# Down projection of a gated MLP: one more pair of row tiles by seven block products

## The reference

```python
h = _L0_tok_ref(...)                                  # 16 x 128 x 1024
h = h + _L0_attn_ref(_layernorm(h), ...)
h = h + _L0_ffn_ref(_layernorm(h), ...)

def _qlinear(x, q, scale, A, Bm):
    w = (q.astype(jnp.float32) - Q_ZERO) * (scale * Q_STEP)[:, None]
    return jnp.einsum('bsh,oh->bso', x, w) + LR_SCALE * (x @ A @ Bm)
g, u = _qlinear(x, gate...), _qlinear(x, up...)       # 2752 hidden features
return _qlinear(silu(g) * u, down...)                 # back to 1024
```

## Time and profile before

| | us |
|---|---|
| median of 3 runs | 1879.42 |
| lowest, highest | 1877.77, 1879.56 |
| the profiled execution's own time | 1879.99 |
| its span | 1878.2 |
| TensorE busy in the span | 1779.6 |
| VectorE busy | 1310.0 |
| GpSimd busy | 977.1 |
| ScalarE busy | 741.9 |

### The profile page before, as it was taken

The page is one execution under the profiler, slowest core; times in us unless marked ns, Lnnn a source line. Parts: engine busy times, 40 slices in busy tenths (PEclk is TensorE's granted clock), DMA queues, the critical chain, the costliest instruction groups (busy, mean ns, idle before and its releaser), DMA issues.

```text
span 1878.2 us, 31695 instructions
## 1 busy us (share of the span) xinstructions
PE 1779.6 (95%) x12772; PEld 970.3 (52%) x12772; DVE 1310.0 (70%) x1758; ACT 741.9 (40%) x1065; POOL 977.1 (52%) x683
## 2 busy tenths in 40 slices
PE   0897999999999999999999999999999999999999
PEld 0786565665666656545554344444444444444444
DVE  8885677777787887855656866775665555377775
ACT  4694334334433444422114544544444443112221
POOL 6881334434334344522360576675668776468672
PEclk9998999999999999999999999999999999999999
DMA  2232111210122221144432333343546453633531
GB/s 100 54 87 68 45 58 17 66 36 21 49 76 65 77 61 62 68 156 166 163 117 79 101 109 127 108 128 101 180 146 207 150 164 104 229 106 141 175 116 68
DMA packets 102705, 194.93 MB, mean 104 GB/s; under 512 B 14304, under 2 KB 75488, under 8 KB 92064
## 3 DMA queue, kind: packets, MB, share of 16 engines
q1 hardware_dynamic: 102560, 192.90, 32.1%
HBM read 135.72 MB, written 56.11 MB: 102 GB/s over the span
## 4 chain that ended last, share of the span: by engine, by line
PE 75%; DVE 10%; POOL 3%; issue 2%; ACT 2%; DMA 0%; DVEq 0%; ACTq 0%
PE acc L1572 13%; PE acc L1574 13%; PE acc L1740 9%; PE acc L1705 4%; PE ps_p L1364 4%; PE ps_p L1366 3%; PE ps_p L1365 3%; PE acc L1478 3%; PE acc L1480 3%; PE acc L1479 3%; PE ps_t L1391 3%; PE ps_p L1380 2%; PE ps_p L1381 2%; PE ps_p L1382 2%; PE ps_l L1581 2%
## 5 line engine op out<-in xcount | busy, mean ns | idle before, releaser
L1218 POOL TENSOR_TENSOR prob<-prob,mx 128x1024 f32<-128x1024 f32 x64 | 121.4, 1898 | 365.6 <-DVE mx L2169 365.6
L1364 PE MATMUL ps_p<-x_hi,w_qk 128*128 128x512 f16 x512 | 194.7, 380 | 0.0
L1365 PE MATMUL ps_p<-x_lo,w_qk 128*128 128x512 f16 x512 | 194.0, 379 | 0.0
L1366 PE MATMUL ps_p<-x_hi,w_qk 128*128 128x512 f16 x512 | 194.0, 379 | 0.0
L1271 POOL TENSOR_TENSOR hidden<-up,hidden 128x512 f16<-128x512 f32 x80 | 91.1, 1161 | 142.3 <-ACT hidden L1998 142.1
L1223 POOL TENSOR_TENSOR prob<-prob,sm 128x1024 f32<-128x1024 f32 x64 | 120.2, 1897 | 52.9 <-DVE sm L2176 52.9
L1380 PE MATMUL ps_p<-w_v,x_hi 128*128 128x256 f16 x512 | 140.4, 274 | 4.1 <-PEq L916 2.8
L1832 ACT ACTIVATE pth<-ps_t 128x512 f16<-128x512 f32 x128 | 76.1, 595 | 163.8 <-PE ps_t L1391 163.7
L1381 PE MATMUL ps_p<-w_v,x_hi 128*128 128x256 f16 x512 | 140.3, 274 | 0.0
L1382 PE MATMUL ps_p<-w_v,x_lo 128*128 128x256 f16 x512 | 140.3, 274 | 0.0
L2421 DVE SCALAR_TENSOR_TENSOR up<-acc,gu_scale,up 128x512 f32<-128x512 f32 x120 | 90.0, 750 | 61.5 <-PE acc L1574 61.0
(11 more groups left out here) (399 smaller groups left out, 4546.1 us busy)
## 6 DMA issues: line engine op xcount, KB each, us to landing
q_raw<-in_gu_q SPq DMA_DIRECT2D x42, 1024.0 KB, 6.2
hid_parts<-hidden_parts SPq DMA_DIRECT2D x16, 1376.0 KB, 7.0
hidden_parts<-hidden SPq DMA_DIRECT2D x42, 512.0 KB, 3.5
down_raw<-in_down_q SPq DMA_DIRECT2D x22, 512.0 KB, 3.6
w_raw<-in_w_qk SPq DMA_DIRECT2D x8, 1024.0 KB, 4.8
h_tokens<-n_tok SPq DMA_DIRECT2D x16, 512.0 KB, 3.7
o_parts<-ot SPq DMA_DIRECT2D x32, 256.0 KB, 2.3
wv_raw<-in_w_o SPq DMA_DIRECT2D x8, 1024.0 KB, 4.9
```

What stands on the lines that cost most here:

```text
L1218: nc.gpsimd.tensor_tensor(prob[s % 2][p][:], prob[s % 2][p][:], bc(mx[p][:], H, 2), ALU.subtract).then_inc(s_sub[p], 1)
L1364: nc.tensor.matmul(out[:], w[:, j % 2, m, 0, at], xn_hi[:, k, tok], start=(k == 0), stop=False)
L1365: nc.tensor.matmul(out[:], w[:, j % 2, m, 0, at], xn_lo[:, k, tok], start=False, stop=False)
L1366: last = nc.tensor.matmul(out[:], w[:, j % 2, m, 1, at], xn_hi[:, k, tok], start=False, stop=(k == KT - 1))
```

## The change

`PLAIN_PAIRS` becomes 1. Row tiles 2 and 3 leave the plain rows and become the first seven-product pair, q = 1, ahead of the six that were there. On GpSimd pair 0 now runs `residual_and_term(0)`, `hid_one(1)`, `hid_three(1)`, `residual_and_term(1)`. On ScalarE the four `down_term` of rows 0 and 1 stand ahead of the high parts of the hidden sums. On VectorE `level_sum(2)` moves ahead of `add_first(0)` and of the hidden sums, and `level_sum(4)` stands right behind `scale_sums(1)`.

```diff
-PLAIN_PAIRS = 2
+PLAIN_PAIRS = 1
@@ GpSimd
         for q in range(DP):
             sums = PLAIN_PAIRS <= q + 1 < DP
+            if q < PLAIN_PAIRS:
+                residual_and_term(2 * q)
             if sums:
                 hid_one(q + 1, 0)
                 hid_one(q + 1, 1)
-            residual_and_term(2 * q)
+            if q >= PLAIN_PAIRS:
+                residual_and_term(2 * q)
@@ ScalarE
             down_term(2 * q, 1)
+            if q < PLAIN_PAIRS:
+                down_term(2 * q + 1, 0)
+                down_term(2 * q + 1, 1)
             if sums:
                 high_hid_sum(q + 1, 0, f1[:], s_f1, 2)
                 high_hid_sum(q + 1, 1, f2, s_f2, 1)
-            down_term(2 * q + 1, 0)
-            down_term(2 * q + 1, 1)
+            if q >= PLAIN_PAIRS:
+                down_term(2 * q + 1, 0)
+                down_term(2 * q + 1, 1)
@@ VectorE
-        for n in range(2):
-            scale_sums(n)
-            add_first(n)
+        scale_sums(0)
+        dve.wait_ge(s_half, 1)
+        for i in range(KD):
+            dve.wait_ge(s_l3, i + 1)
+            tt(level_sum(2, i), level_sum(3, i), level_block(0, 0, i), ALU.add).then_inc(s_l2, 1)
+        add_first(0)
         sum_two_hid(PLAIN_PAIRS)
         sum_two_low(PLAIN_PAIRS)
         low_hid_sum(PLAIN_PAIRS, 0, f1[:])
         low_hid_sum(PLAIN_PAIRS, 1, f2)
-        scale_sums(2)
-        add_first(2)
-        dve.wait_ge(s_half, 1)
-        for i in range(KD):
-            dve.wait_ge(s_l3, i + 1)
-            tt(level_sum(2, i), level_sum(3, i), level_block(0, 0, i), ALU.add).then_inc(s_l2, 1)
-        scale_sums(3)
+        scale_sums(1)
         for i in range(KD):
             dve.wait_ge(s_l2, i + 1)
             tt(level_sum(4, i), level_block(1, 0, i), level_sum(2, i), ALU.subtract).then_inc(s_l4, 1)
-        add_first(3)
+        add_first(1)
```

## The result

| | us |
|---|---|
| before, median of 12 runs | 1878.51 |
| after, median of 12 runs | 1884.26 |
| ratio, 95% interval | 1.0029, 1.0021 to 1.0037 |
| profiled execution after: span | 1881.5 |

One of the twelve executions after took 3796 us; it is counted in the median and left out of the ratio. The changed kernel is slower by 5.75 us in the medians. The interval of the ratio, times 1878.5, is 3.9 to 7.0 us. The two profiled spans are only 3.3 us apart, because this execution reached the down stage 2.06 us earlier: the chain's first 32 matmuls of the stage start at 1591.35, against 1593.41 before.

What follows compares the result with a forecast made beforehand. TensorE, busy 95% of the span, was taken as the bound. Saving 4.3 us, p7 starting 10.0 later (+5.7), and +0.3 for store and clock gave +6.0 on 1879.42: 1885.4 us, range 1877.5 to 1890.0.

Steps and rivals of the forecast that it cites:

- the walk: Engine lists followed through the new first pair to p7: 10.0 us later, less 4.3 saved; +4 to +8 us, chance 0.48.
- The saving of 4.3 us: TensorE, down stage: two plain rows of 38.10 us replaced by one seven-product pair of 33.79, if nothing waits.
- Turns one to one: VectorE's level sums alternate with GpSimd's adds, 1.54 us a turn: level_sum(2) takes 13.7 us, level_sum(4) 8.5, not 3.5 each.
- The wait before p22: TensorE in the new pair stands 6.9 us for scale_sums(1), ready at 1644.1 where p22 wanted it at 1637.2.
- The wait before p7: TensorE stands another 3 us for VectorE's read v at 1661.6; about 1.4 if the clock falls after the first stall.
- the slow clock: TensorE's clock falls after the first stall, costing about 1.5 us, absorbed because p7 waits for VectorE anyway.
- the late store: Row 1's later store may hold x22, which writes the same buffer: at most +0.7 us, within +0.3 shared with the clock.
- a second fall: TensorE's clock falls again after the wait before p7, which would add its cost; within +0.3 us shared with the store.
- The adds are not held up: Rival: level_sum(2) and level_sum(4) take 3.5 us each, nothing waits, 1875.1 us; chance 0.13.
- partly held up: Rival: two VectorE adds per turn, level_sum(2) about 8.5 us, level_sum(4) 5.5; 1877, up to 1880 us; chance 0.21.
- GpSimd goes first: Rival: level_sum(2) and level_sum(4) run only after GpSimd's lists, 1888.1 us; chance 0.18 shared with clock and store.

Runs made afterwards that it cites:

- Run 4: Changed kernel with GpSimd's hid_three(1) waiting for level_sum(2) and hid_one(2) for level_sum(4), VectorE's order kept; ratio 1.0003 against the kernel before.
- run 9: Changed kernel with level_sum(2) and level_sum(4) as three adds each in place of ten, nothing moved, no GpSimd wait; ratio 1.0007 against the kernel before.
- run 1: Changed kernel with scale_sums(1) moved on VectorE to just behind add_first(0), nothing else; ratio 1.0032 against the kernel before.
- run 2: Changed kernel with level_sum(4) moved on VectorE from behind scale_sums(1) to behind the read x5 of pair 1; ratio 1.0035 against the kernel before.
- run 10: Changed kernel with GpSimd waiting for both level sums and ScalarE's copy of p1 between the high parts of f2 and f3; ratio 0.9995 against the kernel before.
- run 8: Changed kernel with ScalarE's copy of p1 ahead of the high part of f2, nothing else; ratio 1.0036 against the kernel before.
- run 3: Changed kernel with scale_sums(1) behind add_first(0) and level_sum(4) behind the read x5; ratio 1.0031 against the kernel before.
- run 11: Changed kernel: three-add level sums, level_sum(4) behind sum_two_low of pair 2, hid_three(1) after level_sum(2), p1 copy between f2 and f3 high parts; 0.9987 against kernel before.
- run 12: As run 11, with GpSimd's residual_and_term(1) moved between the two halves of hid_three(1); ratio 0.9983 against the kernel before, median 1874.71 us.

## Why the prediction was right, point by point

The forecast was 1885.4 and the median is 1884.26; against the kernel before, +6.0 and +5.75. The kernel is slower, by about what the walk gave, and by its mechanism. Of the 1.1 us between forecast and median, 0.9 lie in the kernel before, whose median was 1879.42 over 3 executions and 1878.51 over 12.

- *The saving of 4.3 us.* Right: 38.10 us of two plain rows became one pair. The pair took 43.47 us (TensorE's row at 1630.39 to the one at 1673.86, by its timeline), 9.68 more than the undisturbed 33.79, and 9.68 - 4.31 = 5.37 is the stage's +5.33.
- *Turns one to one.* Right. Predicted 13.7 us for level_sum(2) and 8.5 for level_sum(4), measured 13.4 (1620.17 to 1633.53) and 8.7 (1641.44 to 1650.11). Run 4, which takes GpSimd away, and run 9, which takes the instructions away, each give back most of what level_sum(2) lost (4.25 and 5.8 us in place of 13.4). The Trainium skill ("SBUF — State Buffer", "Who interferes with whom") has the exclusion of a VectorE instruction with two SBUF inputs and a GpSimd instruction that reads SBUF; that the waiting VectorE add gets in after each single GpSimd add is what these runs show.
- *The wait before p22.* Predicted 6.9, recorded 6.58. Right, but no cause by itself: runs 1 and 2.
- *The wait before p7.* Predicted 3 us, or about 1.4 with the slow clock; it was 0.34. Here the clock was the mis-sized term. From p22's start to p5's start TensorE took 12.63 us (1641.67 to 1654.30); in run 10, without a wait there, 10.18 (1634.21 to 1644.39), as in the kernel before. The fall cost 2.45 us, not 1.5, which is what it cost behind the shorter wait of run 9 (1.55). That hid nearly all of the second wait and changed nothing in the sum, since v comes when VectorE is done: predicted 1661.6, or 1659.5 with the earlier start of the stage, and 1658.98 measured. So the 0.5 us by which VectorE was ahead, and the +0.3 for the late store and a second fall, neither of which happened (x22 follows c11 at once at 1656.09), are about what the forecast was too high by (+6.0 against +5.33 in the stage).
- *What the walk did not see.* The copy of p1. It took part in none of the numbers of this kernel, since the wait for it lies behind the one of p22 (run 8), but it was a third chain, also set off by level_sum(2). It made the longest wait of TensorE in runs 1, 3 and 4. That it did not spoil the forecast is luck: nothing in the walk says that it is no longer than the others. The prediction looked at ScalarE's list only for whether its parts were covered, not for what was queued behind them.
- *The rivals.* "The adds are not held up" and "partly held up" fall by the rows of line 2625. "GpSimd goes first" falls by the same rows: the first six adds came in between. The 9.7 us that the new pair loses are thus three chains from one cause, nearly of one length; undoing any one of the waits alone wins nothing (runs 1, 2, 8), and taking the cause away wins 3.6 to 5 us (runs 9 and 4).

What stays open: runs 11 and 12 have 2.5 of the 4.3 us. 1.4 to 1.5 of the rest is the wait before p4, which run 12's order of GpSimd's list did not remove; other orders were not tried. The last 0.3 to 0.5 us were not followed up.

## What to carry to other kernels

An engine with 15 us of idle time can still be the wrong place for ten small adds, if the engine beside it has a list of its own that it must take turns with: count its instructions, not its idle time, and then make few wide instructions or let one engine wait. When a stage is moved earlier, walk every engine's list up to the last deadline, since one late step holds several chains, and the trace names only the one that ends last. Repairs have to be made together, and each has to be checked for what it now puts in front of something else.

## What the runs showed of the hardware

- Adds of VectorE with both inputs in SBUF, beside adds of GpSimd, take turns by instruction: ten adds of 128x512 took 13.4 us, three adds with the same elements 5.8 us, and 4.25 us when GpSimd waited.
- TensorE's clock fell after rather short waits. Waits of 2.7 us (run 9) and 2.8 us (run 4) were followed by stretches of 4 us with a granted clock of 0.64 (1636 to 1640) and 0.63 (1640 to 1644); after waits of 0.96 and 1.88 us (run 10) every stretch to 1660 stood at 1.00, and so did those around the waits of 2.00 us in run 1 (1656 to 1664) and 2.18 us in run 3 (1664 to 1672). The row of run 9:

```profile
1636.00:1640.00 4.00, 2.62 (x7) 1.00 (x8) 4.00 (x4) 0.00 (x0) 3.79 (x3) 0.64 0.74 259
```

The fall after run 9's wait cost 1.55 us (p22's start to p5's start, 1637.38 to 1649.11, against the 10.18 of run 10).
